# First cross-attention on one NeuronCore: scores from high and low parts of queries and keys

## What is computed

```python
q = (ln @ Wq).reshape(b, m, h, d)                 # m = 112 queries, h = 8 heads, d = 64
kv_x, kv_l = xn @ Wkv, ln @ Wkv                   # 375 context rows, 112 latent rows
k_x = rope_rotate_k(k_x)                          # only context keys are rotated
k = jnp.concatenate([k_x, k_l], axis=2)           # 487 keys
sim = jnp.einsum('bhid,bhjd->bhij', q * scale, k)
out = jnp.einsum('bhij,bhjd->bhid', softmax(sim), v)
```

## Time and profile before

| | |
|---|---|
| median of 3 runs | 744.95 us (744.82 to 746.98) |
| profiled execution | 744.0 us, span 742.2 us |
| granted TensorE clock | 1.0 throughout |
| busy | PE 715.7 us (96%), DVE 530.4 (71%), ACT 446.1 (60%), POOL 191.9 (26%) |
| first cross-attention | about 24 to 242 us of the span |

### The profile page before, as it was taken

The page is one execution under the profiler, slowest core; times in us unless marked ns, Lnnn a source line. Parts: engine busy times, 40 slices in busy tenths (PEclk is TensorE's granted clock), DMA queues, the critical chain, the costliest instruction groups (busy, mean ns, idle before and its releaser), DMA issues.

```text
span 742.2 us, 15906 instructions
## 1 busy us (share of the span) xinstructions
PE 715.7 (96%) x5594; PEld 588.0 (79%) x5594; DVE 530.4 (71%) x1266; ACT 446.1 (60%) x1203; POOL 191.9 (26%) x317
## 2 busy tenths in 40 slices
PE   9999999999998999999999999988999999899998
PEld 8567777777766788999999987766777767889988
DVE  2798787888678320777787748668788886897754
ACT  3676667667656513677777754677878787112131
POOL 4132231212000043011001017645454547201000
PEclk9999999999999999999999999999999999999999
DMA  5322333333111478477766623510000000000001
GB/s 170 101 79 68 78 95 102 106 103 92 42 31 24 134 252 302 137 255 252 226 212 213 206 79 93 184 57 3 2 2 2 2 2 1 1 1 1 1 7 43
DMA packets 43537, 69.81 MB, mean 94 GB/s; under 512 B 6611, under 2 KB 35036, under 8 KB 43204
## 3 DMA queue, kind: packets, MB, share of 16 engines
q1 hardware_dynamic: 41924, 65.14, 28.0%
q0 software_dynamic: 1536, 3.67, 1.5%
HBM read 52.56 MB, written 8.26 MB: 82 GB/s over the span
## 4 chain that ended last, share of the span: by engine, by line
PE 82%; DVE 8%; ACT 4%; issue 3%; DMA 2%; POOL 1%; SPq 0%; POOLq 0%; ACTq 0%; DVEq 0%
PE ps L1530 12%; PE ps L1798 10%; PE ps L1815 8%; PE ps L2017 7%; PE ps L1592 5%; PE ps L1595 5%; PE ps L1634 4%; PE ps L1899 4%; PE ps L1654 3%; PE ps L1843 3%; PE ps L1722 3%; PE ps L1853 3%; PE ps L2052 2%; PE ps L1605 2%; PE ps L1535 2%
## 5 line engine op out<-in xcount | busy, mean ns | idle before, releaser
L1530 PE MATMUL ps<-ident,arena 112*122 112x112 f32 (+5 forms) x584 | 81.6, 274 | 5.9 <-ACT rt L864 3.8
L1530 PEld LDWEIGHTS ps<-ident,arena 112*122 112x122 f32 (+5 forms) x584 | 63.5, 154 | 29.4 <-issue 14.7
L1034 DVE TENSOR_REDUCE negmax<-ps 112x1 f32<-112x375 f32 x128 | 61.2, 540 | 29.6 <-PE ps L1899 29.6
L820 ACT ACTIVATE arena_r<-ps,bt 128x128 fp32r<-128x128 f32 x168 | 70.1, 419 | 18.0 <-PE ps L1798 18.0
L1798 PE MATMUL ps<-OT,arena 128*128 128x128 f32 x672 | 78.5, 275 | 0.6 <-issue 0.6
L2017 PE MATMUL ps<-arena_r 128*112 128x384 f32 x384 | 75.9, 346 | 1.9 <-DVE acc L1319 1.0
L1798 PEld LDWEIGHTS ps<-OT,arena 128*128 128x128 f32 x672 | 76.7, 192 | 0.9 <-issue 0.8
L821 ACT ACTIVATE OT<-ps,bt 128x128 f32<-128x128 f32 x168 | 71.1, 425 | 0.0
L2017 PEld LDWEIGHTS ps<-arena_r 128*112 128x112 f32 x384 | 63.8, 175 | 4.0 <-DVE arena L1452 1.2
L1029 DVE TENSOR_REDUCE negmax<-ps 112x1 f32<-112x487 f32 x64 | 39.5, 658 | 22.7 <-PE ps L1634 22.7
L679 ACT ACTIVATE arena<-ps,negmax 112x487 f32<-112x487 f32 x64 | 42.7, 670 | 15.3 <-DVE negmax L1029 15.3
(11 more groups left out here) (312 smaller groups left out, 1692.2 us busy)
## 6 DMA issues: line engine op xcount, KB each, us to landing
arena<-in_up_w SPq DMA_DIRECT2D x21, 1024.0 KB, 5.1
arena<-in_down_w SPq DMA_DIRECT2D x8, 1024.0 KB, 6.5
arena<-arena SPq DMA_DIRECT2D x128, 60.9 KB, 2.0
arena<-in_wqkv SPq DMA_DIRECT2D x1, 3072.0 KB, 10.3
arena<-in_ctx SPq DMA_DIRECT2D x8, 375.0 KB
slot_rows<-acc SPq DMA_DIRECT2D x6, 448.0 KB, 3.5
OT<-slot_rows SPq DMA_DIRECT2D x21, 128.0 KB, 2.7
slot_out<-yo SPq DMA_DIRECT2D x21, 128.0 KB, 2.8
```

What stands on the lines that cost most here:

```text
L820: act.activation(he_hi[:, i % 2, m, :], src, ACT.Gelu, bias=bt[:, i % 3, m:m + 1])
L1034: dve.tensor_reduce(negmax[0:TQ, h % 4:h % 4 + 1], ps[0:TQ, S_BANKS[h % 4], 0:TK], AX, ALU.max, negate=True)\
L1530: return pe.transpose(dst, src, ident[0:k, 0:k])
```

## The change

Queries and rotated keys are split into high and low parts, and each pair of float32 score products becomes three pairs of one-pass products: q_hi·k_hi, q_lo·k_hi, q_hi·k_lo. For that:

- ACT's `l0_q` copies the query result twice, into `q_hi` and `qh`; POOL's new `q_low` subtracts, once a batch (128x448).
- DVE's `l0_rope` gets a fourth instruction, the cast into `kr_hi` (128x487); POOL's new `kr_low` makes the low part from two SBUF inputs (128x487), once a unit. For unit 0 DVE makes it itself.
- PE's scores wait for `q_low` (once a batch), and the third pair for `kr_low`.
- Keys have two slots, i mod 2, in place of four.

Three semaphores are merged into another one to free their numbers, with no other effect. The diff, cut to its core:

```diff
@@ POOL
+            def kr_low(i):
+                pool.wait_ge(L0["ke"], i + 1)
+                pool.tensor_tensor(kr_lo[:, i % 2, 0:NK0], kr[:, i % 2, 0:NK0], kr_hi[:, i % 2, 0:NK0].bitcast(F32), ALU.subtract)\
+                    .then_inc(s_krlo, 1)
+
+            def q_low(n):
+                pool.wait_ge(L0["qe"], n + 1)
+                pool.tensor_tensor(q_lo[n % 2], qh[n % 2], q_hi[n % 2].bitcast(F32), ALU.subtract).then_inc(s_qlo, 1)
+
+            pool.tensor_copy(kr_pad[:, :, NK0:NKP0], wT[:, 0:4].unsqueeze(2))
+            q_low(0)
             for n in range(B):
                 if n and n + 2 < B:
                     latents_rstd(n + 2, 0)
+                kr_low(4 * n + 1)
+                if n and n + 2 < B:
                     latents_rstd(n + 2, 1)
+                kr_low(4 * n + 2)
                 if n + 2 < B:
                     ctx_rstd(n + 2)
                 if n == 0:
                     latents_rstd(2, 0)
+                kr_low(4 * n + 3)
+                if n == 0:
                     latents_rstd(2, 1)
+                if n + 1 < B:
+                    q_low(n + 1)
+                    kr_low(4 * n + 4)
                 if n:
                     rows_rstd(n - 1)
@@ ACT, l0_q
-                act.activation(qh[p].rearrange("p h q -> p (h q)"), ps[:, l0_bank("q", n, 0), 0:4 * TQ], ACT.Copy, scale=0.125)\
+                src = ps[:, l0_bank("q", n, 0), 0:4 * TQ].rearrange("p (c q) -> p c q", c=4)
+                act.activation(q_hi[p], src, ACT.Copy, scale=0.125)
+                act.activation(qh[p], src, ACT.Copy, scale=0.125)\
                    .then_inc(L0["qe"], 1)
@@ DVE, l0_rope
-                if n:
-                    dve.wait_ge(L0["s"], (n - 1) * H0 + 2 * m + 2)
-                k, w = kr[:, m, 0:NK0], ksw[i % 2][:, 0:NK0]
+                if i >= 2:
+                    dve.wait_ge(L0["s"], 2 * i - 2)
+                k, w = kr[:, i % 2, 0:NK0], ksw[i % 2][:, 0:NK0]
                 link(dve.tensor_tensor(k, kraw[i % 2][:, 0:NK0], cos_t[:, :], ALU.mult))
                 dve.wait_ge(s_ksw[i % 2], 64 * (i // 2 + 1))
                 link(dve.tensor_tensor(w, w, sin_t[:, :], ALU.mult))
-                dve.tensor_tensor(k, k, w, ALU.add).then_inc(L0["ke"], 1)
+                link(dve.tensor_tensor(k, k, w, ALU.add))
+                dve.tensor_copy(kr_hi[:, i % 2, 0:NK0], k).then_inc(L0["ke"], 1)
+                if i == 0:
+                    dve.wait_ge(L0["ke"], 1)
+                    dve.tensor_tensor(kr_lo[:, 0, 0:NK0], k, kr_hi[:, 0, 0:NK0].bitcast(F32), ALU.subtract)\
+                       .then_inc(s_krlo, 1)
@@ PE, l0_s
+                for k, (qv, kv) in enumerate(((q_hi, kr_hi), (q_lo, kr_hi), (q_hi, kr_lo))):
+                    if k == 2:
+                        pe.wait_ge(s_krlo, i + 1)
+                    for r in (0, 1):
+                        rows = slice(64 * r, 64 * r + 64)
+                        ins = pe.matmul(ps[0:TQ, r, 0:NKP0], qv[p][rows, u, :], kv[rows, i % 2, :], start=(k == 0),
+                                        stop=(k == 2), tile_position=(64 * r, 0))
+                        if k == 2:
+                            ins.then_inc(L0["s"], 1)
```

More of the change, by code:

```diff
@@ L175, in build @@
         (kv_hi, kv_lo, wkv_hi, wkv_lo) = layout(21760, [P, KC, NKP0], [P, KC, NKP0], [P, KC, 1024], [P, KC, 1024], of=arena_r)
+        kr_lo, kr_hi = layout(9120, [P, 2, NKP0], [P, 2, NKP0], of=arena_r)
+        (kr_pad,) = layout(9120, [P, 4, NKP0], of=arena_r)
+        q_hi = layout(17120, [P, 4, TQ], [P, 4, TQ], of=arena_r)
+        q_lo = tuple(OT_r[:, 1792 + k * 4 * TQ:1792 + (k + 1) * 4 * TQ].rearrange("p (c q) -> p c q", c=4) for k in (0, 1))
         cx, hat, kvin = (cx_0, cx_1), (hat_0, hat_1), (kvin_0, kvin_1)
-        kraw, ksw, v0, qh = (kraw_0, kraw_1), (ksw_0, ksw_1), (v_0, v_1), (qa_0, qa_1)
+        kraw, ksw, v0 = (kraw_0, kraw_1), (ksw_0, ksw_1), (v_0, v_1)
         (kT, vc, vm_0, vm_1, qt, qm_1, probs1, pT1,
@@ L224, in build @@
         flat = OT[:, :, :].rearrange("p c q -> p (c q)")
+        qh = tuple(flat[:, 1792 + k * 4 * TQ:1792 + (k + 1) * 4 * TQ].rearrange("p (c q) -> p c q", c=4) for k in (0, 1))
         ot0 = flat[:, 2688:3584].rearrange("p (k c q) -> p k c q", k=2, c=4)
@@ L239, in build @@
         s_seen = sem("waits_seen")
-        s_tanh = sem("gates_tanh")
+        s_tanh = sem("gates_tanh_exp_and_squares")
         s_lstat, s_lrstd, s_ln = sem("latents_stats"), sem("latents_rstd"), sem("latents_normed")
@@ L253, in build @@
         L0 = ring("l0", "t1 q k v t1e qe ke ve s max exp rinv norm pt pte pv ote")
-        s_kraw = sem("l0_k_copied")
+        s_kraw, s_krlo, s_qlo = sem("l0_k_copied"), sem("l0_k_low_parts"), sem("l0_q_low_parts")
         s_kvhi, s_kvlo, s_shlo = sem("high_parts"), sem("l0_kv_low_parts"), sem("shared_low_parts")
@@ L285, in build @@
         s_wt, s_wte = sem("wT_done"), sem("wT_ready")
-        s_gsq, s_gpow, s_gz, s_gexp = (sem(n) for n in ("squares_ready", "gating_norms", "gating_z", "gating_exp"))
-        s_sge = sem("gates_exp")
+        s_gpow, s_gz, s_gexp = (sem(n) for n in ("gating_norms", "gating_z", "gating_exp"))
         (s_xb, s_m, s_mx, s_qkv, s_qk, s_qkTe, s_sc, s_scm, s_nm, s_ex, s_ri, s_p2, s_p2e, s_o, s_att, s_mixd, s_mt,
@@ L735, in l0_step @@
                     act.activation(tgate[:, :], gate[:, :], ACT.Tanh).then_inc(s_tanh, 1)
-                    act.activation(sgate[:, :], gates[:, :], ACT.Exp, scale=-1.0).then_inc(s_sge, 1)
+                    act.activation(sgate[:, :], gates[:, :], ACT.Exp, scale=-1.0).then_inc(s_tanh, 1)
                 if u < 2:
@@ L844, in rowsT_out @@
                    .then_inc(s_xte, 1)
-            act.activation(simsq[:, :, :], simm[:, :, :], ACT.Square).then_inc(s_gsq, 1)
+            act.activation(simsq[:, :, :], simm[:, :, :], ACT.Square).then_inc(s_tanh, 1)
             for n in range(B):
@@ L1321, in gate_const @@
             def gate_const():
-                dve.wait_ge(s_sge, 1)
+                dve.wait_ge(s_tanh, 2)
                 dve.wait_ge(s_gpow, 1)
@@ L1625, in l0_s @@
             def l0_s(n, p, u):
-                g = n * H0 + 2 * u
+                g, i = n * H0 + 2 * u, 4 * n + u
                 if u == 0:
-                    pe.wait_ge(L0["qe"], n + 1)
-                pe.wait_ge(L0["ke"], 4 * n + u + 1)
+                    pe.wait_ge(s_qlo, n + 1)
+                pe.wait_ge(L0["ke"], i + 1)
                 if g:
                     pe.wait_ge(L0["exp"], g)
-                for r in (0, 1):
-                    rows = slice(64 * r, 64 * r + 64)
-                    pe.matmul(ps[0:TQ, r, 0:NK0], qh[p][rows, u, :], kr[rows, u, 0:NK0], start=True, stop=True,
-                              tile_position=(64 * r, 0)).then_inc(L0["s"], 1)
+                for k, (qv, kv) in enumerate(((q_hi, kr_hi), (q_lo, kr_hi), (q_hi, kr_lo))):
[7 more added lines that the diff above has]
+                            ins.then_inc(L0["s"], 1)
             def l0_pt(g, h):
@@ L1958, in l1_g @@
                 if n == 0:
-                    pe.wait_ge(s_gsq, 1)
+                    pe.wait_ge(s_tanh, 3)
                     for c in range(KC):
```

## The result

The changed kernel takes 763.58 us (median, 760.84 to 764.96), the kernel before 744.92 us beside it: 1.023 times as long (95% interval 1.021 to 1.025), 2.3% slower. The forecast was 768 us within 750 to 781.

A forecast was written before the change was run, and what follows sets the result against it. PE was taken to bound the kernel, DVE to become the bound: 15 (batches 1 to 5) + 6.4 and 0.6 (batch 0 and ahead) + 0 (batch 6) + 1.9 (batch 7) = +23.9 on 744.95, said as 768 us, range 750 to 781.

The forecast's parts named there:

- DVE becomes the bound: Batches 1 to 5: DVE needs 30.7 us a batch against 27.74 now and some 27.1 of PE, +15 us.
- The hold: POOL's low part of the keys holds DVE's norm 1.06 us a unit, 4.24 a batch; `q_low` adds 0.9 a batch.
- PE's pairs: Score products: six one-pass records take 0.85 us a unit in place of 1.00, saving 0.15 a unit, 0.6 a batch.
- The cast: DVE, once a unit: 0.41 us plus 0.03 for the wait on its own result, 1.76 a batch.
- POOL's prices: POOL's low-part subtractions: 1.23 us for 487 columns of keys, 1.14 for 448 columns of queries.
- PE waits for the cast, not for the low part: Scores: the third pair can run 1.3 us after the cast, and DVE is held longer than that.
- Waits for swapped keys vanish: DVE's waits for swapped keys, 6.9 us over batches 1 to 5 before the change, go away.
- Batch 0: Already DVE-bound: 24.7 us needed grow to 31.6 against 25.15, +6.4 us.
- Batch 7: PE's wait for the last rotation grows by cast and low part, +1.3, plus +0.6 for a held norm: +1.9 us.
- The room of 3.9 us a batch: DVE's waits in batches 1 to 5, 19.5 us; given more than 3.9 a batch, DVE becomes the bound.
- holds of half the size: 753: Rival, chance 0.15: holds of 0.5 us a unit, a batch asks 28.0 us of DVE, kernel takes 753 us.

The follow-up runs named there:

- e2: Changed kernel without any low parts of keys or queries, all score pairs taking the high parts; 745.99 us, 1.0009 of before.
- e6: Kernel before with six one-pass products of high parts a unit, rounded keys written by DVE's add, no cast; 743.63 us, 0.9924 of before.
- e1: Changed kernel with the third score pair taking high parts again, so not waiting for POOL's low part, which is still made; 761.02 us.
- e11: Changed kernel with POOL's low part of the third unit's keys waiting for DVE's second norm of that step; 762.55 us, 1.0230 of before.
- e8c: Kernel before plus POOL writing 1344 columns of unused zeros when a unit's keys are ready, except each batch's third unit; 751.90 us.
- e8d: Kernel before plus POOL writing 1344 columns of unused zeros when a unit's keys are ready, except each batch's second unit; 749.81 us.
- e5: Changed kernel without low parts and with the two float32 score products of before; 756.43 us, 1.0102 of before.
- e4: Changed kernel with all low parts of the keys made on DVE behind the cast, not on POOL; 757.02 us, 1.0147 of before.
- e8: Kernel before plus POOL writing 1344 columns of unused zeros whenever a unit's keys are ready; 758.20 us, 1.0116 of before.

## Why the prediction came out right, and where its steps were off

**DVE becomes the bound**: shown. Half of the chain of batches 1 to 5 runs over DVE, and e2 gives the time back when nothing is held. A batch was forecast from a need of 30.7 us; it takes 29.6 in the mean of batches 1 to 5.

**The hold** of 1.06 us a unit: the mechanism was right, the size of the term a fifth too large. Held norms took 1.46 to 1.49 us against 0.47, so 1.0 each, in three units of a batch. The fourth, the batch's second unit, is not held, since another DVE instruction stands behind its cast:

```profile
178.86 0.41 DVE L1020 TENSOR_SCALAR xn<-x,mv,rstd 112x256 f32<-112x256 f32 x1
...
179.02 1.33 POOL L484 TENSOR_TENSOR arena_r<-arena,arena_r 128x487 fp32r<-128x487 f32 x1 [0.81 <-DVE arena_r L1051]
...
180.03 0.59 DVE L1072 TENSOR_SCALAR arena<-arena,rinv 112x488 f32<-112x488 f32 x1
```

Here DVE is first by 0.16 us and keeps its 0.41; statistics follow, which are not held, and the norm loses 0.12. `q_low` holds the second norm for 0.70 (1.17 us), not 0.9. The sum is 3 x 1.0 + 0.12 + 0.70 = 3.8 us a batch where I had 4.24 + 0.9 = 5.1. With it the need is 23.8 + 1.8 + 3.8 = 29.4 us, and four of the five batches took 28.80, 29.78, 29.39 and 29.37, 29.3 in the mean. This is the mis-sized term: +9.5 us for batches 1 to 5, not +15. (A slip beside it: the rotation and norm instructions that show no stretch before the change are 96 and 64, not some 190.)

**PE's pairs**: 0.85 us a unit was forecast from the 1.00 of the earlier trace rows; by the timeline six records take 0.91 to 0.92 from the first start to the last end where four took 1.07. Saved: 0.16 us against 0.15, and e6 gives 0.65 a batch. That a float32 record runs at half the one-pass rate, on which the 0.85 rests, has its row in the trace of before: eight records of 256 columns (L1605) take 1.89 us, 0.24 each, where a one-pass record of 488 takes 0.22. **The cast**: 0.41 and 0.03, as forecast. **POOL's prices**: 1.24 us for the keys (1.23), 1.31 for the queries (1.14; the two that start with no norm running take 1.14).

**"PE waits for the cast, not for the low part"** failed as put: between the products 4.1 us for the low part and 2.4 for the cast, with the weight loads 15.1 and 7.5. At the second unit of a running batch the norm is not held, PE asks right behind the cast, and its score products start 1.1 us before the low part is there; at the third unit they start 1.0 us after it. But e1 shows that these waits are worth 2.1 us in all, because DVE is late behind them anyway.

**Waits for swapped keys vanish**: from 8.5 us between 50 and 200 us to 1.4.

**Batch 0** +4.3 us, forecast +6.4, by the same smaller hold, and with a piece that no term of the forecast had, TensorE's clock. PE's timeline and two windows of the changed kernel:

```profile
43.49 2.81 PE L1622 MATMUL ps<-arena_r 128*128 128x488 f32 x6 [1.98 <-DVE arena_r L1111]
...
73.31 2.23 PE L1622 MATMUL ps<-arena_r 128*128 128x488 f32 x6 [2.13 <-DVE arena_r L1111]
...
66.00:72.00 6.00, 5.18 (x50) 4.17 (x48) 5.72 (x15) 3.87 (x9) 1.99 (x3) 1.00 0.26 51
72.00:78.00 6.00, 4.69 (x14) 3.48 (x16) 5.83 (x10) 2.60 (x8) 4.71 (x5) 0.72 0.13 34
```

In batches 0 and 1 PE waited 1.98 and 2.13 us for DVE's low part of the inputs, behind the third unit's held norm, and then worked at half clock (0.72 in the mean of 6 us, 1.00 in the window before). e11 frees just that norm: there the windows 42 to 48 and 66 to 78 us have 1.00, and batches 0 and 1 take 58.6 us together, not 60.4. Batches 2 to 6 gain 1.5 us more, and batch 7 loses 1.1 again, at half clock from 242.1 to 252.3 us. Batch 1's 30.87 us is the clock too: in e1 PE waits 2.47 us at the same place, the clock stays at 1.00, and the batch takes 29.05. **Batch 7** +4.9, forecast +1.9. Here the forecast had PE wait for the cast and the low part, which it does, but not what came of it:

```profile
247.70 0.48 PE L1667 MATMUL ps<-arena_r 64*112 64x488 f32 x2 [1.80 <-DVE arena_r L1051]
248.02 0.53 PE L1667 MATMUL ps<-arena_r,OT_r 64*112 64x488 f32 x2
249.00 0.74 PE L1667 MATMUL ps<-arena_r 64*112 64x488 f32 x2 [0.46 <-POOL arena_r L484]
249.68 1.76 PE L1689 MATMUL ps<-arena 122*64 122x112 f32 x16
251.37 1.75 PE L1560 MATMUL ps<-ident,arena 112*122 112x112 f32 x8
252.91 2.89 PE L1635 MATMUL ps<-arena,OT 128*112 128x256 f32 x8
```

The last three take 0.99, 0.98 and 1.89 us at full clock; 2.5 us went to the half clock. So overestimates of 5.5 us (batches 1 to 5) and 2.1 (batch 0) and an underestimate of 3.0 (batch 7) partly cancelled, and the forecast was nearer than its terms: in that part it was luck.

**The room of 3.9 us a batch** decided nothing here, since the need went far over it, but as a way to count it failed: e8c had DVE need 26.8 of 27.8 us and lost 0.7 us a batch, e8d had it need 26.7 and lost nothing in its usual batches. The rival "holds of half the size: 753" rested on that count too. The room lies in single steps, and in the second step (second unit's scores to the third's) the one hold on the standardising is more than there is.

## What to carry to other kernels

Work given to an idle GpSimd is not free for a VectorE that runs fast one-input instructions (scalings, casts) at that moment. Look at what VectorE does in the microsecond after the release; statistics and maxima were not held by reads (none met a long write), scalings were held, by reads and writes alike. Here doing the same work on VectorE itself was 6.6 us cheaper.

Count an engine's room by step, not by batch or by its busy share, and follow a held instruction to the one that waits last. And take a long wait away for a test before blaming it, and look whether it is counted at the products or at the weight loads ahead of them: 15.1 us of waits were 4.1 between products, and worth 2.1.

## What the runs showed of the hardware

- A POOL instruction that only writes (1344 columns of zeros, 1.22 us) held a one-input DVE scaling of 488 columns for 0.97 us, as one with two inputs of 487 columns did (0.99).
- DVE scalings whose records start 0.03 and 0.05 us behind POOL's were held, and let go 0.2 us before POOL's recorded end; one that starts 0.16 us ahead of POOL's subtraction was not, and one that starts 0.14 us ahead of its zeros was (1.51 us in place of 0.41).
- After single waits of PE of 1.45, 1.98, 2.13 and 3.30 us, and after 1.80 with 0.46 soon behind it, at full clock until then (2.4 GHz), the next products ran at half of it (1.2 GHz; 0.50 granted in a whole window of e5, 303 to 306 us). In the changed kernel's trace this happened three times, and it makes a late producer cost more than the wait itself. It doesn't follow every such wait: behind 2.47 us in e1 (to 73.2 us) and 2.17 in e6 (to 294.9 us) the clock stayed at full, and behind the 1.7 us ahead of the shared expert it fell in three traces (e4, e8, e8d) and stayed in the others.
- Three pairs of one-pass products in the two halves of the array, 488 columns each, take 0.91 to 0.92 us, two pairs of float32 ones 1.07.
